# ScalarE's order in a softmax attention loop: the next image's exponential ahead of the copies of the present image's turned probabilities

## The reference

```python
Q = _apply_rope(jnp.einsum('bsd,ed->bse', x, wq), cos, sin)
K = _apply_rope(jnp.einsum('bsd,ed->bse', x, wk), cos, sin)
V = jnp.einsum('bsd,ed->bse', x, wv)
...
scores = jnp.einsum('bhqd,bhkd->bhqk', Q, K) / math.sqrt(DIM_K)
weights = jax.nn.softmax(scores, axis=-1)
out = jnp.einsum('bhqk,bhkd->bhqd', weights, V)
```

## Time and profile before

| | |
|---|---|
| median of 3 runs | 1179.62 us (1175.94 to 1181.26) |
| the profiled execution | 1180.71 us, its span 1178.9 us |
| TensorE busy over the span | 973.6 us (83%) |
| VectorE, ScalarE, GpSimd busy | 643.8, 576.6, 647.4 us |
| the stage `attention()` | about 125 to 278 us |

### The profile page before, as it was taken

One profiled execution on the slowest core, in us unless ns is written; L12 is line 12 of the kernel. 1 busy time (PEld: TensorE's weight loads), 2 busy tenths in 40 slices (PEclk: granted clock), 3 DMA queues, 4 the chain that ended last, 5 costly groups with the idle time before them and its releaser, 6 DMA issues. The chain is left out here.

```text
span 1178.9 us, 21890 instructions
## 1 busy us (share of the span) xinstructions
PE 973.6 (83%) x6860; PEld 868.1 (74%) x6860; DVE 643.8 (55%) x1439; ACT 576.6 (49%) x1175; POOL 647.4 (55%) x623
## 2 busy tenths in 40 slices
PE   6269699997899999688887799993199999999970
PEld 5258377776788988466666699992199999999970
DVE  1335599994465563499996355543633333333335
ACT  0021277775355565333443456652166676666640
POOL 0115488875355553244333699861167777777750
PEclk9679899997799999878888799995589999999995
DMA  7661344441111111000000600007246666666656
GB/s 249 181 248 50 86 139 158 157 159 44 54 55 55 55 55 55 1 0 1 0 0 9 283 2 14 28 15 279 99 140 197 194 205 182 204 193 202 198 169 230
DMA packets 64749, 136.93 MB, mean 116 GB/s; under 512 B 12361, under 2 KB 26434, under 8 KB 63346
## 3 DMA queue, kind: packets, MB, share of 16 engines
q1 hardware_dynamic: 55698, 113.32, 29.8%
q0 software_dynamic: 4848, 14.72, 3.6%
q10 hardware_dynamic: 4144, 8.16, 1.9%
HBM read 114.01 MB, written 24.39 MB: 117 GB/s over the span
## 5 line engine op out<-in xcount | busy, mean ns | idle before, releaser
L121 DVE CAST place<-place 128x512 fp32r<-128x512 f32 (+3 forms) x188 | 107.4, 609 | 176.0 <-PE moe_down L127 100.5
L2273 POOL TENSOR_TENSOR place<-place,place 128x512 fp32r<-128x512 f32 x84 | 138.3, 1646 | 52.2 <-DVE place L121 52.2
L2299 PE MATMUL moe_up<-place,place 128*128 128x128 f32 x1376 | 163.3, 278 | 0.0
L2299 PEld LDWEIGHTS moe_up<-place,place 128*128 128x128 f32 x1376 | 159.8, 195 | 0.0
L127 PE MATMUL moe_down<-place,place 128*128 128x256 f32 x1008 | 130.8, 286 | 0.0
L127 PEld LDWEIGHTS moe_down<-place,place 128*128 128x128 f32 x1008 | 123.3, 191 | 0.0
L2358 ACT ACTIVATE place<-place 128x2048 f32 x44 | 84.0, 1912 | 44.0 <-PEq L2095 29.9
L2371 ACT ACTIVATE place<-moe_up,place 128x128 f32<-128x128 f32 x344 | 97.5, 366 | 15.2 <-POOL place L2273 14.7
L1423 POOL TENSOR_TENSOR place<-place,place 128x384 fp32r<-128x384 f32 x42 | 43.7, 1043 | 89.3 <-ACT place L1330 62.4
L1528 POOL TENSOR_TENSOR place<-place,place 69x1024 f32<-69x1024 f32 x16 | 30.9, 1929 | 93.1 <-DVE place L167 93.1
L785 PE MATMUL scores<-place,place 128*69 128x276 f32 x256 | 68.5, 412 | 11.1 <-DVE place L849 6.8
(11 more groups left out here) (271 smaller groups left out, 2128.5 us busy)
## 6 DMA issues: line engine op xcount, KB each, us to landing
place<-w_remainder SPq DMA_DIRECT2D x172, 256.0 KB, 4.0
place<-in_w_dram SPq DMA_DIRECT2D x4, 4096.0 KB, 12.9
place<-gate_rows SPq DMA_DIRECT2D x24, 384.0 KB, 4.8
place<-in_w_dram SPq DMA_DIRECT2D x16, 512.0 KB, 3.8
w_remainder<-place SPq DMA_DIRECT2D x16, 512.0 KB, 3.0
place<-value_rows SPq DMA_DIRECT2D x64, 64.0 KB, 2.8
place<-choices ACTq DMA_DIRECT2D x5, 768.0 KB, 7.1
place<-in_patches_dram SPq DMA_DIRECT2D x9, 384.0 KB, 3.8
```

Of the source, the lines that this page charges most:

```text
L121: return eng.tensor_copy(out, x)
L2273: pool.tensor_tensor(lo[f], raw[f], hi[f].bitcast(F32), ALU.subtract).then_inc(h_split, 1)
L2299: last = pe.matmul(p1[u][k // HK][:, (k % HK) * P:(k % HK + 1) * P], ws[u][:, c, k * P:(k + 1) * P], xT[u][:, c, :], start=(c == 0), stop= ...
```

## The change

In ScalarE's list for image n, the exponential of image n+1 is put first and the copies of the turned probabilities of image n second. Everything else stays.

```diff
                 for n in range(NB):
-                    copy_probs(n)
                     if n + 1 < NB:
                         exp(n + 1)
+                    copy_probs(n)
                     if n >= 1:
                         copy_out(n - 1)
```

## The result

The changed kernel takes 1208.45 us (median of 4 runs, 1207.90 to 1208.59); the kernel before, run beside it, 1178.95 (1175.94 to 1181.26). The ratio is 1.0251, 95% interval 1.0227 to 1.0275: slower by 29.5 us, where 26.4 were forecast (1207).

The account below looks back on a forecast made before the run. TensorE was taken to bound the attention stage. 15 x 1.15 for cut images, 14 x 0.57 for plain ones and 1.15 for image 30 made 26.4 us, added to 1180.71: 1207 us, range 1200 to 1232.

Parts of the forecast that it names:

- TensorE is the bound, and ScalarE's idle time is behind the copies: Attention stage: TensorE busy 39.22 of 40 us; ScalarE idle 25.4 us in 115 before `set_values`, waiting for TensorE's last L813.
- row: Stretch of 29 images from the L813 of image 0 to that of image 29, 121.92 us in the kernel before.
- The exponential waits for nothing, and nobody waits for it: ScalarE's L894 and L895: inputs ready 0.34 us early, output 0.59 us before its reader; cost 0, gain 0.
- The VectorE rival: VectorE's late L849 would hold the exponential and so the copies, giving 1209 or 1216 us; chance 0.04.
- 1.15 us in a cut image, 0.57 in a plain one: Late copies delay L810: 1.15 us where ScalarE cuts part of w2 before the image, 0.57 where it does not.
- the cover: In a plain image L810 could have gone 0.58 us earlier, so that much of the copies' delay costs nothing.
- The sum: Over the images: 15 x 1.15 + 14 x 0.57 + 1.15 for image 30, together 26.4 us.
- W: The end of the last L813 of an image on TensorE, from which the image's loop is timed.
- the end of the stage: Last images of attention: 1.15 us for image 30, without scores to cover the copies; 0 for image 31.
- The clock rival: TensorE's clock falls in the new idle gaps: 3 to 10 images add 9 to 29 us, 1225 for six; chance 0.26.
- My price of 2.9 us an image: Extra time of an image with TensorE at the low clock, over the 5.06 us mean of the new images.
- The other side: The exponential rides in ScalarE's idle time and the copies lose nothing: 1178 to 1180 us, not slower; chance 0.04.

Follow-up runs that it names:

- the early cut: The kernel before with ScalarE's cut of w2 moved ahead of the setting of the values: 1178.00 us, ratio 0.9992.
- The runs with half of the change: Two runs against the kernel before, exponential ahead of the copies only in even images (1192.01 us) or only in odd ones (1210.61 us).
- the short part alone: The kernel before with only the short part of the exponential (L894) put ahead of the copies: 1180.25 us, ratio 0.9999.
- the cut images alone: The kernel before with the exponential ahead of the copies only in odd images, those behind a cut of w2: 1210.61 us, ratio 1.0256.
- the new waits: The changed kernel with TensorE's waits ahead of L810 reordered, those for the copies last, and no idle products: 1207.37 us, ratio 1.0246.
- these gaps filled: The changed kernel with two idle products in TensorE's gap of odd images and its waits for the copies last: 1202.41 us, ratio 1.0209.
- changed, cut early: The changed kernel with ScalarE's cut of w2 moved ahead of the setting of the values: 1191.14 us, ratio 1.0101.

## Why the prediction was right, by its steps

*TensorE is the bound, and ScalarE's idle time is behind the copies.* Right. Moving the cut into that time took 16.3 us of row from the changed kernel; moving the exponential out of it added 27.2 (2.2 of either are the two falls of the clock).

*The exponential waits for nothing, and nobody waits for it.* Right: after the change L894 has 0.3 us of idle time ahead of it in 27 images, from 150 to 290 us. The VectorE rival did not happen here. VectorE's small reserve at 4.0 us an image was real though: it took the gain of the early cut.

*1.15 us in a cut image, 0.57 in a plain one.* 1.12 (5.51 for 4.39) and 0.56 (4.57 for 4.01) were measured. The runs with half of the change show each term alone, and the short part alone shows the cover.

*The sum.* 15 x 1.12 + 14 x 0.56 = 24.6 us for the row, 25.2 forecast. The row grew by 27.2. The rest is two falls of the clock, in images 2 and 18, of about 1.1 each, and 0.3 in image 10. There `set_values` (L913) starts 0.38 us behind W and not 0.11. The kernel before has the same delay (its copies of image 10 end 0.57 ahead of L810, where the other plain images have 0.84), but there it lies under the cover. What holds L913 back is not shown. The images after the row were put at 1.15 and cost 2.1: the clock was low from the L810 of image 30 on, whose L813 now took 2.01 us (1.43 before). That the total came within 1.5 us is in part luck. The falls (2.2), image 10 (0.3) and the end of the stage (1.0 over its term), some 3.5 us that the sum did not have, stand against 0.6 too much in the row and 2.2 less outside it, and the forecast started from the profiled execution, 1.1 over the median. The terms for an image do not need that luck.

*The clock rival.* I gave it 0.26 as something that hits 3 to 10 images or does not. It hit two, and the time stayed with the forecast. But three kernels with nearly the same gaps in their cut images had two, six and five falls (the changed one, the cut images alone, the new waits), and with these gaps filled there was none. What decides between two falls and six is not shown, and I could not have told the number from the rows of before. My price of 2.9 us an image was too high for a fall that lasts less than an image: 1.1 to 1.65. By the rule of the Trainium skill that I had set beside it ("TensorE: Matmul & The Clock Gate", Why this matters for your kernels) the clock would have held in gaps as short as these; it fell at gaps of 1.3 us and less, and the measurement decides.

*The other side* did not happen, for the reason given: the idle time stands ahead of `set_values`.

## What to carry to other kernels

Idle time of an engine says where work can be put only together with its place in the queue: 1.1 us of work cost 1.1, 0.56 or nothing here, by the two hand-overs between which it stood. Before filling such a gap, look at what the moved step releases on a third engine, since that work may block a fourth. And where an engine waits on several semaphores, try the one that comes last at the end; it was worth 0.11 us each time here.

## What the runs showed of the hardware

With a gap of 1.2 to 1.3 us ahead of L810 in every second image, TensorE's granted clock went down to about half now and then (two, five and six times in 29 images); with two small products in that gap it stayed at 1.00 through the row. With gaps of 0.38 us in every image (changed, cut early) it did not fall either. The order of TensorE's waits was worth 0.11 us each time the late one was not the last: L810 started 0.25 us behind the end of the last copy, and 0.14 with the new order. And a VectorE operation with two SBUF inputs (L858) that was held by a GpSimd instruction ended some 0.28 us after that instruction, wherever the two met: 0.41 us became 0.56 in the kernel before, and 0.72, 1.07, 1.11 and 1.52 in the others.
